# A decoder layer in float32: the next tile's y products at the end of a step, and the second normalisation turned by VectorE squares and DMA transfers instead of TensorE transposes

## The reference

```python
x = x + self_attention(layernorm(x))          # blocks of 128 rows, causal, one head of width 512, with a bias
x = x + cross_attention(layernorm(x), ctx)    # 16 heads of 32, 64 keys a batch, silu in place of softmax, mask
x = x + ffn(layernorm(x))                     # 512 -> 2048 -> 512, exact gelu
```

## Time and profile before

| | us |
|---|---|
| median of 3 runs (lowest to highest) | 1253.47 (1253.17 to 1254.33) |
| the profiled execution, its own time | 1254.45 |
| its span in the profile | 1252.7 |

### The profile page before, as it was taken

One profiled execution on the slowest core, in us unless ns is written; L12 is line 12 of the kernel. 1 busy time (PEld: TensorE's weight loads), 2 busy tenths in 40 slices (PEclk: granted clock), 3 DMA queues, 4 the chain that ended last, 5 costly groups with the idle time before them and its releaser, 6 DMA issues.

```text
span 1252.7 us, 15584 instructions
## 1 busy us (share of the span) xinstructions
PE 1238.3 (99%) x5672; PEld 1029.7 (82%) x5672; DVE 689.0 (55%) x1238; ACT 488.9 (39%) x888; POOL 245.2 (20%) x226
## 2 busy tenths in 40 slices
PE   9997999999999999999999999999999999999998
PEld 7886888888888888878888888888888888888887
DVE  7777878787878776957643333424424333334211
ACT  7354555656464656554232222222322222322221
POOL 2223223232323222258302001001001020010000
PEclk9998999999999999999999999999999999999999
DMA  8432222222222120335110020010100100100000
GB/s 295 149 107 67 90 66 91 79 78 80 75 80 75 46 75 18 120 108 178 35 68 1 1 68 1 6 61 0 67 0 0 67 0 0 67 0 0 34 1 33
DMA packets 60649, 74.75 MB, mean 60 GB/s; under 512 B 6464, under 2 KB 31040, under 8 KB 60608
## 3 DMA queue, kind: packets, MB, share of 16 engines
q1 hardware_dynamic: 60608, 74.22, 18.6%
HBM read 48.51 MB, written 18.35 MB: 53 GB/s over the span
## 4 chain that ended last, share of the span: by engine, by line
PE 55%; DVE 0%; issue 0%; DVEq 0%
PE bank L53 18%; PE bank L55 18%; PE bank L54 18%; DVE resid L1405 0%; DVEq L1404 0%
## 5 line engine op out<-in xcount | busy, mean ns | idle before, releaser
L1395 DVE TENSOR_TENSOR hid_lo<-gelu_out,hid_hi 128x512 fp32r<-128x512 f32 x128 | 98.1, 766 | 403.8 <-ACT gelu_out L1359 403.7
L53 PE MATMUL bank<-zT,w_parts 128*128 128x512 f32 x752 | 293.0, 390 | 2.7 <-DVE qo_lo L833 1.9
L54 PE MATMUL bank<-zT,w_parts 128*128 128x512 f32 x752 | 292.6, 389 | 0.0
L55 PE MATMUL bank<-zT,w_parts 128*128 128x512 f32 x752 | 292.6, 389 | 0.0
L1355 ACT ACTIVATE hid_hi<-bank,small 128x512 fp32r<-128x512 f32 x128 | 88.3, 690 | 498.6 <-PE bank L55 498.6
L53 PE MATMUL bank<-w2p_hi,hid_lo 128*128 128x512 f32 x512 | 199.2, 389 | 0.0
L54 PE MATMUL bank<-w2p_lo,hid_hi 128*128 128x512 f32 x512 | 199.2, 389 | 0.0
L55 PE MATMUL bank<-w2p_hi,hid_hi 128*128 128x512 f32 x512 | 199.2, 389 | 0.0
L53 PEld LDWEIGHTS bank<-zT,w_parts 128*128 128x128 f32 x752 | 141.1, 188 | 33.3 <-DVE qo_lo L833 2.4
L54 PEld LDWEIGHTS bank<-zT,w_parts 128*128 128x128 f32 x752 | 141.3, 188 | 29.2
L55 PEld LDWEIGHTS bank<-zT,w_parts 128*128 128x128 f32 x752 | 141.0, 188 | 29.4
(11 more groups left out here) (155 smaller groups left out, 1838.7 us busy)
## 6 DMA issues: line engine op xcount, KB each, us to landing
x_in<-in_x SPq DMA_DIRECT2D x32, 256.0 KB, 3.6
x_dram<-resid SPq DMA_DIRECT2D x32, 256.0 KB, 2.1
raws<-in_w SPq DMA_DIRECT2D x32, 256.0 KB, 3.2
resid<-x_dram SPq DMA_DIRECT2D x32, 256.0 KB, 3.7
out_dram<-resid SPq DMA_DIRECT2D x32, 256.0 KB, 2.1
raws<-in_x SPq DMA_DIRECT2D x28, 256.0 KB, 3.5
z_cols<-raws SPq DMA_DIRECT2D x112, 64.0 KB, 2.0
resid<-in_wqkvT SPq DMA_DIRECT2D x12, 256.0 KB, 5.1
```

The lines of the kernel that those rows point to most:

```text
L53: pe.matmul(out_ap, lhs[1], rhs[0], start=start, stop=False)
L54: pe.matmul(out_ap, lhs[0], rhs[1], start=False, stop=False)
L55: return pe.matmul(out_ap, lhs[0], rhs[0], start=False, stop=stop)
L1395: dve.tensor_tensor(hid[1][:, c % 4, :], gelu_out[:, c % 2, :], f(hid[0][:, c % 4, :]), ALU.subtract).then_inc(hid_lo, 1)
```

## The change

On PE the four `y_rows` of the next tile move from behind the queries to the end of the step before, behind the output shares, and all four output shares now stand together. In steps 0 to 6 the 16 transposes of z2 are gone. Instead DVE turns z2 in squares (`turn2`, into `scratch`, which is act_in and prob in one tensor), and 16 transfers carry the squares into `z1_cols`: SP issues 8 and ACT issues 8. ACT and DVE then make z2's parts in `attn`, which the queries read. Step 7 keeps the transposes. zT is free after the values of a step, so z1 of the next tile goes there at the step's end, ahead of the transfers of z2. Some banks are dealt out anew, and the lists of PE and ACT unroll two more steps.

```diff
-VALUE_BANK = (5, 6, 7, 0)
+VALUE_BANK = (0, 6, 7, 5)
-PROB_BANK = 5
+PROB_BANK = 0
-OUT_BANK = (7, 0, 1, 5)
+OUT_BANK = (7, 5, 1, 0)
+Y_BANK = (2, 3, 4, 6)
...
+            def move_squares(engine, source, rows, moved):
+                for r in rows:
+                    for q in range(QUADS):
+                        engine.dma_start(z1_cols[cols(q, SQUARE), :, :]..., source[cols(r, SQUARE), 0:NB, :]...
+                            ).then_inc(moved, 16)
...
 # SP, step
-                                else:
-                                    sp.wait_ge(z1T_lo, EC * (a + 1))
+                                move_squares(sp, raws, range(QUADS), z1_moved)
...
+                            if more(a):
+                                sp.wait_ge(z2_turned, NB * (a + 1))
+                                move_squares(sp, scratch, range(QUADS // 2), z2_moved)
+                            if b is not None:
+                                store_x2(b, 1 - par)
...
 # ACT, step: the front
                                 for m in range(EC - 1):
                                     q_high(b, m)
-                                if not first(b):
-                                    act.wait_ge(z1_moved, MOVES * a)
-                                    act.wait_ge(q_done, EC * (b + 1))
-                                    z1_high(0)
                                 q_high(b, EC - 1)
-                                if not first(b):
-                                    for c in range(1, EC):
-                                        z1_high(c)
 # ACT, step: the end
+                            if more(a):
+                                if b is not None:
+                                    z1_high_now(a + 1)
+                                act.wait_ge(z2_turned, NB * (a + 1))
+                                move_squares(act, scratch, range(QUADS // 2, QUADS), z2_moved)
+                                y_high(a + 1, 0)
+                                y_high(a + 1, 1)
+                                act.wait_ge(z2_moved, MOVES * (a + 1))
+                                for c in range(EC):
+                                    act.activation(by_blocks(attn[0], c), by_quads(c), ACT.Copy).then_inc(z2T_hi, 1)
+                                y_high(a + 1, 2)
+                                y_high(a + 1, 3)
...
 # DVE
+                        def turn2(a, b):
+                            dve.wait_ge(z2_ready, NB * (a + 1))
+                            if b is not None:
+                                dve.wait_ge(attn_lo, PAIRS * (b + 1))
+                            dve.nop(nofuse=True)
+                            for i in range(NB):
+                                dve.transpose(turned2[:, :, i, :], zn[:, i, :]...).then_inc(z2_turned, 1)
...
+                            if more(a):
+                                for c in range(EC):
+                                    z1_low(a + 1, c)
+                                norm_rows(dve, lambda i: x1_rows(i, par), mv2, rstd2, ln2, a)
+                                turn2(a, b)
+                                if b is not None:
+                                    for i in range(3):
+                                        second_residual(dve, b, i, 1 - par)
+                                if twice_more(a):
+                                    stats_ahead(dve, a + 2, (0, 1))
+                                if b is not None:
+                                    second_residual(dve, b, 3, 1 - par)
+                                y_low(a + 1, 0)
+                                if twice_more(a):
+                                    stats_ahead(dve, a + 2, (2, 3))
+                                    aggregate(dve, a + 2, mv1, ln1)
+                                y_low(a + 1, 1)
+                                for c in range(EC):
+                                    z2_low(a, c)
+                                y_low(a + 1, 2)
+                                y_low(a + 1, 3)
...
 # PE, step
-                                    last = product(pe, bank[m][:, :], at(wqk, c, cols(m)), at(zT, c),
-                                                   c == 0, c == EC - 1)
...
-                            if b is not None:
-                                pe.wait_ge(s2_masked, PAIRS * b + 2)
                             value_rows(0)
                             pe.wait_ge(y_lo, EC * (a + 1))
+                            if b is not None:
+                                pe.wait_ge(s2_masked, PAIRS * b + 1)
+                                pe.wait_ge(q_lo, 2 * EC * (b + 1))
...
+                            if more(a):
+                                pe.wait_ge(x1_ready, NB * (a + 1))
+                                pe.wait_ge(z1T_lo, EC * (a + 2))
+                                for m in range(EC):
+                                    y_rows(a + 1, m)
                             else:
                                 for i in range(NB):
                                     transposed_rows(pe, z2_ready, a, i, BLOCK_BANK[i], z2T_done)
```

More of the change, by code:

```diff
@@ L550, in y_bank, with proj_bank @@
                 def y_bank(a, m):
-                    return FIRST_Y_BANK[m] if first(a) else m
+                    return FIRST_Y_BANK[m] if first(a) else Y_BANK[m]
+                def proj_bank(a):
+                    return PROJ_BANK if more(a) else END_PROJ_BANK
                 def more(a):
@@ L766, in step @@
                                         ).then_inc(keys_out, 1)
[L767 to L773, removed]
-                                y_high(1, 2)
+                            if more(a):
+                                if b is not None:
+                                    z1_high_now(a + 1)
+                                act.wait_ge(z2_turned, NB * (a + 1))
[7 more added lines that the diff above has]
+                                y_high(a + 1, 3)
                             else:
                                 for i in range(NB):
-                                    transpose_high(act, i, BLOCK_BANK[i], z2T_done, z2T_hi, a)
+                                    transpose_high(act, i, BLOCK_BANK[i], z2T_done, z2T_hi, 0)
                         def last_step(b):
@@ L803, in last_step @@
                             transpose_high(act, 3, FIRST_BANK[3], z3T_done, z3T_hi, 0)
-                        pipeline(act, step, last_step)
+                        pipeline(act, step, last_step, peeled=2)
                     @block.vector
@@ L894, in step @@
                                 if not first(b):
-                                    z1_low(a, 0)
+                                    values_low(b)
                                 q_low(b, EC - 1)
-                                if not first(b):
-                                    for c in range(1, EC):
-                                        z1_low(a, c)
-                                if not first(b):
-                                    values_low(b)
                                 dve.wait_ge(mask_ready, b + 1)
@@ L975, in step @@
                                                   ALU.add).then_inc(x1_ready, 1)
-                            if b is None:
-                                for c in range(EC):
-                                    z1_low(1, c)
                             dve.wait_ge(x1_ready, NB * (a + 1))
@@ L997, in step @@
-                            if b is not None:
-                                second_residual(dve, b, 2, 1 - par)
-                            if first(a):
-                                y_low(1, 0)
-                                y_low(1, 1)
-                                for i in range(NB):
-                                    dve.wait_ge(z2T_hi, i + 1)
-                                    dve.tensor_tensor(attn[1][:, :, cols(i)], chunks(bank[FIRST_Z2_BANK[i]][:, :]),
-                                                      f(attn[0][:, :, cols(i)]), ALU.subtract).then_inc(z2T_lo, 1)
-                                y_low(1, 2)
-                            else:
+                            if more(a):
[19 more added lines that the diff above has]
+                                y_low(a + 1, 3)
+                            else:
+                                next_stats(dve, TILES, (0, 1))
+                                norm_rows(dve, lambda i: x1_rows(i, par), mv2, rstd2, ln2, a)
+                                for i in range(3):
+                                    second_residual(dve, b, i, 1 - par, END_PROJ_BANK)
@@ L1179, in step @@
                                     pe.wait_ge(wo_lo, EC)
-                                for i in range(3):
+                                for i in range(NB if more(a) else 3):
                                     for c in range(EC):
@@ L1243, in last_step @@
                                     output_share(i, c, LAST_PROJ_BANK)
-                        pipeline(pe, step, last_step)
+                        pipeline(pe, step, last_step, peeled=2)
```

128 lines of the change are left out of this document (48 added, 80 removed).

## The result

| | us |
|---|---|
| before, median of 7 runs (lowest to highest) | 1253.73 (1253.17 to 1254.58) |
| changed, median of 7 runs | 1257.76 (1256.65 to 1260.99) |
| ratio, 95% interval | 1.0036 [1.0024, 1.0048] |
| changed, the profiled execution: own time, span | 1257.62, 1255.8 |

The sign of the prediction was wrong; its range held the time. Against its own sum for the profiled execution, 1249.9, the changed kernel is 7.7 us late.

What follows compares the result with a forecast made beforehand. PE was taken as the bound, busy 1238.3 of 1252.7 us. First and second step -5.1, steps 2 to 6 +2.3, step 7 -1.75 sum to -4.55 us, so 1249, range 1243 to 1270.

Steps and rivals of the forecast that it cites:

- The sign of the prediction: Whole kernel: predicted faster, by 4.55 us (-0.36%), with chance 0.52 of faster.
- its own sum: Whole kernel: predicted terms add to -4.55 us, giving 1249.9 for the profiled execution.
- What is removed: PE, steps 0 to 6: z2's transposes go, 1.75 us a step, 12.3 us in all.
- The wait of 2.0 before the self scores: Steps 2 to 6: PE waits 2.0 us for DVE's masked score, five times; none in step 7.
- Two queues at once: z2's transfers: SP and ACT each issue at 0.65 us at the same time, landing after 6.6 us.
- The rival built on it: Step boundaries: transfers go one at a time, the last landing 5.2 us later; 1271, chance 0.16.
- If the five waits of 2.0 did it too, 13.5 more; nothing shorter than 4.72 shows it.: Steps 2 to 6: clock falls at the five waits would add 13.5 us; left out of the sum.
- Landed at 88.0, z2_low at 90.9 ... PE does y from 76.8 to 87.7 and waits 3.2.: First boundary: z2 lands at 88.0, its low parts end at 90.9, and PE waits 3.2 us before the queries.
- The extra 0.2 a step: Steps 2 to 6: the last masked score comes 1.1 us later against 0.87 of slack, another 0.2 us.
- DVE's list has no idle place to give: DVE in repeated steps: argument that its chain to the masked score cannot be shorter than the sum.
- the rival of a shorter chain: Repeated steps: DVE's chain is shorter, so neither 2.0 nor 0.2 is waited; 1238, chance 0.10.
- clock falls in the wait of the first boundary: First boundary: PE's clock falls in the new wait of 3.2 us; 1252, no measurable change, chance 0.12.

Runs made afterwards that it cites:

- e9: e8 with DVE's steps unrolled further (peeled=4), so its loop has no jump back; 1239.35 us.
- e11: e8 with the edits of e9 and e10 together; 1237.63 us, ratio 0.9878 to the kernel before.
- e4: Changed kernel with all 16 transfers of z2 issued by SP, none by ACT; 1277.46 us.
- e2: Changed kernel with only the mask put ahead of the keys' differences on DVE; 1251.66 us.
- e3: Kernel before with only the change's unrolling of two more steps on PE and ACT; 1253.12 us.
- e7: Changed kernel with two extra DVE statistics instructions ahead of masked score 0 in steps 2 to 6, lengthening the wait; 1270.71 us.
- e1: Changed kernel with DVE's rows of the next tile put ahead of the keys' differences in every step; 1248.58 us.
- e5: Changed kernel with the first step's four x loads issued by SP behind its z2 transfers instead of ahead; 1258.28 us.
- e10: e8 with DVE's second pair of statistics and the aggregates of the next tile ahead of y_low 0; 1239.81 us.
- e6: Changed kernel with the edits of e1 and e5, plus the first step's low parts of the values ahead of query 3; 1244.85 us.
- e8: e6 with the mask also ahead of the keys' differences in every step, as in e2; 1240.91 us.

## Why the prediction was wrong

**What is removed: right.** 1.75 a step. In e9 and e11, where nothing hides it, a step takes 59.55 against 61.38 before, 1.8 less.

**The wait of 2.0 before the self scores: right**, in place, size (1.85 to 1.99) and number (five, none in step 7), and so is the chain behind it: undisturbed steps of 61.74 to 61.78 against 61.8.

**Two queues at once: right.** ACT's eight issues and SP's eight start together in the repeated step:

```profile
335.24 5.23 ACTq L262 DMA_DIRECT2D z_cols<-scratch  x8
```

```profile
335.23 5.52 SPq L262 DMA_DIRECT2D z_cols<-scratch  x8
```

0.65 and 0.69 us apart; SP's alone were 0.65. The rule of the Trainium skill (Perfetto Trace Analysis, DMA Instruction — HWDGE (DVE, Sync)), that the generator is locked for one issuer, did not show as a cost here: the trace disagrees with the reading by which the two would queue. The rival built on it, with 1271 for transfers one at a time, is what e4 made, at 1277.46, and its price was near by luck in part: it had 35.8 us of waits (3.2 + 5 x 2.0 + 22.6) where e4 shows 28.7, and nothing for the clock, which cost e4 some 12.

**The failed steps, two.**
- *"If the five waits of 2.0 did it too, 13.5 more; nothing shorter than 4.72 shows it."* The sum priced five waits of 2.0 as 2.0 each and put the clock down to 4.72 only. In the profile of the changed kernel two of five dropped the clock. The two steps are 63.92 + 63.53 - 2 x 61.77 = 3.9 us too long, of the 7.7; 3.1 of this is between self scores and transposes, where the clock is low, and 0.8 is in short pieces behind the transposes before, left unexplained. The profiles show it as a dose: 1.2 us of wait, none of five (e2); 1.9 to 2.0, two of five in two kernels and one in e3; 3.1 to 3.3, four of five (e7); 3.1 to 4.1, six of six (e4). The 13.5 was as wrong: a fall costs 1.7 for 3.41 us, not the 2.7 of the earlier trace rows, and not every wait has one. The number of falls differs from run to run: the seven executions of the changed kernel have a mean granted clock of 0.996 in the fastest (1256.65), 0.992 in the slowest (1260.99), and 0.993 to 0.994 between, in this order; 0.004 of 1257 us is 5 us, as the spread of 4.3 is. e11 has 0.998 to 0.999 and spreads over 0.4. It is not the only source of spread: e1 has 0.997 at 1246.27 and at 1249.31.
- *"Landed at 88.0, z2_low at 90.9 ... PE does y from 76.8 to 87.7 and waits 3.2."* The 6.6 us of the landing came from a share of 0.30, in a step where no loads are under way. With them it was 9.7 us, and the wait 6.15. e5 takes the loads away and gets 87.8 and a wait of 4.70. What is left then is DVE's order, which the late landing had covered: ACT brings up y_high 0 only after its own eight issues, so DVE does nothing for 5.0 us and then puts 2.3 us of statistics and y_low 1 ahead of z2_low. e10 takes that away and gets 3.37. The transposes started at 124.55; the sum has them at 125.50 - 5.1 = 120.4. That is 4.1 us, the clock at this wait included, which the sum put at nothing. e11, with both causes and the values' low parts mended, has them at 119.59.

3.9 + 4.1 = 8.0, against the 7.7 missed; the other way go the undisturbed steps, 61.77 instead of 61.83, five times.

**The extra 0.2 a step** at the last masked score is not to be told apart; undisturbed steps leave no room for more.

**"DVE's list has no idle place to give"**, which the prediction said against the rival of a shorter chain, did not hold: its own sum lets DVE begin start_step only at Y + 4.3, and the trace shows DVE idle for 2.82 us there. e1 uses just this place.

**The rival "clock falls in the wait of the first boundary"** (0.12) was what happened there; that it would reach some of the waits of 2.0 too, it left open.

## What to carry to other kernels

Where TensorE is the bound, price a new wait of about 2 us or more as the wait plus 1.7 us times the chance that the clock falls (two in five at 2.0 us here, four in five at 3.2), and ask of each such wait which work of the late engine can go into idle time just ahead of it: here DVE waited 2.8 us for ACT and then made PE wait 2.0, and one reordering was worth 9 us. A landing time read in one step holds only where the same other transfers are under way. And after each wait removed, look who is next: e5 brought the data 2.7 us earlier, and 0.7 of it reached the transposes.

## What the runs showed of the hardware

- A low granted clock lasted 3.41 or 6.83 us (10.24 once, at the wait of 8.05 in e4), at or behind waits of 1.94 us or longer, and behind none of 1.38 or less in the profiled steps. The same wait of 1.9 had it in e3 and not in the kernel before. In the low stretch matmuls of 512 columns start 0.427 us apart (e3, 102.54 to 105.10) and not 0.227. The Trainium skill (TensorE: Matmul & The Clock Gate, What's actually happening) gives two levels only; the trace agrees, and all mean clocks between are mixtures.
- SP and ACT issued side by side, 0.65 to 0.69 us for each move of 64 KB, where SP alone took 0.65.
- At the one jump back of DVE's loop DVE stood still for 2.36 to 2.41 us, in five kernels (e1, e2, e6, e8, e10); unrolled, it is gone in two (e9: 1.6 us of the time; e11 against e10: 2.2). Why the jump costs this was not tried. In the changed kernel DVE waits there for the keys (2.82 us), so the gap would be hidden.
- The values' differences on DVE beside POOL take 4.17 us for four, against 1.24 without, as before.
